# A four-layer graph network on one core: layer 0's gathered rows as three 16-bit pieces

## The reference, cut to what matters

```python
h = jnp.maximum(_layernorm(x, axis=-1), 0.0)
x = x + _L0_gnn_ref(h, edge_attr_128, src, dst, L0_gnn_W, L0_gnn_b, L0_gnn_We, L0_gnn_be)
# _L0_gnn_ref(nfeat, efeat, ...):
    h = nfeat * norm_src[:, None]                     # norm_src = out_degree ** -0.5
    agg = jax.ops.segment_sum(h[src], dst, num_segments=N)
    conv = agg @ W * norm_dst[:, None] + b
    sfeat = (nfeat @ W + b) / (in_deg + 1.0)[:, None]
    e = efeat @ We + be
    esum = jax.ops.segment_sum(e, dst, num_segments=N)
    return conv + sfeat + esum / jnp.clip(in_deg, 1.0, None)[:, None]
```

## Time and profile before

| | us |
|---|---|
| median of three runs | 7222.97 |
| lowest, highest | 7200.09, 7244.32 |
| span of the profiled execution | 7221.2 |

### The profile page before, as it was taken

How to read it: one execution, slowest core, us unless ns; L and a number is a source line. 1 busy time by engine, 2 the same in 40 slices (tenths; PEclk the granted TensorE clock), 3 DMA queues, 4 the chain that set the end, 5 groups by cost and what they waited for, 6 DMA issues and landing times. The chain is left out here.

```text
span 7221.2 us, 86037 instructions
## 1 busy us (share of the span) xinstructions
PE 4312.1 (60%) x19030; PEld 3495.4 (48%) x19030; DVE 3856.8 (53%) x11927; ACT 1462.0 (20%) x3928; POOL 4096.8 (57%) x4194
## 2 busy tenths in 40 slices
PE   4577777846656565795666666333344446556565
PEld 4466666635555555443444444233333345555554
DVE  7344444446666556745555555244444446556665
ACT  4122222212222222361111111000000112222222
POOL 1566666646666565006666665666666556555653
PEclk9877767666666666897888888555655566676766
DMA  2433333323333334164444445122222433333333
GB/s 49 125 99 101 100 100 101 100 89 105 106 108 108 105 108 87 64 279 140 130 136 128 136 129 117 52 55 61 59 56 59 72 100 107 110 113 105 113 115 64
DMA packets 426871, 738.64 MB, mean 102 GB/s; under 512 B 100571, under 2 KB 280628, under 8 KB 419797
## 3 DMA queue, kind: packets, MB, share of 16 engines
q0 software_dynamic: 173296, 436.67, 23.0%
q1 hardware_dynamic: 244484, 289.62, 12.3%
q10 hardware_dynamic: 8592, 6.82, 0.4%
HBM read 613.74 MB, written 120.20 MB: 102 GB/s over the span
## 5 line engine op out<-in xcount | busy, mean ns | idle before, releaser
L1619 POOL DMA_INDIRECT xh<-pair_d,src_i x1658 | 1653.2, 997 | 1181.9 <-issue 457.1
L2630 POOL DMA_INDIRECT l2e_rows<-msg_d,msg_i x829 | 807.1, 974 | 744.7 <-POOLq L61 316.8
L986 POOL DMA_INDIRECT l0e_rows<-node_d,src_i x832 | 793.9, 954 | 465.0 <-issue 220.6
L841 POOL DMA_INDIRECT l2f_rows<-msg_d,msg_i x829 | 787.0, 949 | 428.4 <-issue 231.2
L1141 PE MATMUL l0e_ps<-l0e_rows,l0e_sel 128*128 128x256 f32 x1664 | 787.1, 570 | 304.1 <-issue 187.3
L875 PE MATMUL l2f_ps<-l2f_rows,l2f_sel 128*128 128x128 f32 x1664 | 403.8, 409 | 597.2 <-DVE xh L906 482.6
L2748 PE MATMUL l2e_ps<-l2e_rows,l2e_sel 128*128 128x256 f32 x1664 | 485.8, 424 | 423.2 <-DVE l2e_sel L2842 406.4
L875 PEld LDWEIGHTS l2f_ps<-l2f_rows,l2f_sel 128*128 128x128 f32 x1664 | 359.1, 304 | 671.3 <-issue 409.6
L2807 DVE TENSOR_TENSOR l_acc<-l_acc,l2e_ps 128x256 f32 x832 | 349.2, 420 | 511.5 <-DMA node_d<-l1t_queries 347.7
L1206 DVE TENSOR_TENSOR early_acc<-early_acc,l0e_ps 128x264 f32 x832 | 356.6, 429 | 470.7 <-PE l0e_ps L1142 181.6
L906 DVE TENSOR_TENSOR xh<-xh,l2f_ps 128x128 f32 x832 | 238.2, 286 | 676.3 <-DMA tb_raw<-edges_d,starti 466.7
(11 more groups left out here) (454 smaller groups left out, 8155.1 us busy)
## 6 DMA issues: line engine op xcount, KB each, us to landing
l0e_rows<-in_edge_attr_dram SPq DMA_DIRECT2D x832, 64.0 KB
msg_d<-l1t_queries SPq DMA_DIRECT2D x50, 1024.0 KB, 3.9
l1te_local<-local_d SPq DMA_DIRECT2D x52, 512.0 KB
l2e_local<-local_d SPq DMA_DIRECT2D x52, 512.0 KB
l3te_local<-local_d SPq DMA_DIRECT2D x52, 512.0 KB
xh<-pair_d,src_i POOLq DMA_INDIRECT x1658
msg_d<-l2e_msg SPq DMA_DIRECT2D x50, 512.0 KB
l0e_rows<-node_d,src_i POOLq DMA_INDIRECT x832
```

Source lines behind the costliest of these rows:

```text
L841: pool.indirect_dma_start(rows[:, t % R, :], None, table, bass.IndirectOffsetOnAxis(index[:, t:t + 1], 0)) \
L986: pool.indirect_dma_start(rows[:, t % R, 0:D], None, table, bass.IndirectOffsetOnAxis(g.src_i[:, t:t + 1], 0)).then_inc(gathered[t % R], 16)
L1619: pool.indirect_dma_start(rows[:, t % R, :], None, g.pair_d, bass.IndirectOffsetOnAxis(g.src_i[:, t:t + 1], 0)).then_inc(gathered[n % RG], 16)
L2630: pool.indirect_dma_start(rows[:, t % R, :], None, table, bass.IndirectOffsetOnAxis(index[:, t:t + 1], 0)).then_inc(gathered[t % R], 16)
```

## The change

Table: a row of `node_d` becomes 384 16-bit numbers (768 bytes) instead of 128 32-bit ones (512 bytes): the value split into a head, a middle and a tail piece whose sum is exact, stored in the order middle, tail, head. After a slot is scaled, ScalarE copies the head to 16 bits, VectorE subtracts it, ScalarE copies the middle, VectorE writes the tail; SyncE sends the slot after its tail. The order on ScalarE is: (scale k,) head of k, middle of k-1; on VectorE: take the head from k, tail of k-1, scale k+1.

Pass: the ring is two, `near` (16-bit, 384 columns of pieces and 8 of relations, which `choose` now writes there) and `far` (32-bit, the edge features). Per tile PE makes one 16-bit product of 136 columns (head and relations), two of 128 columns that add to it, all with `narrow` as the stationary operand, and one 32-bit product of 128 columns. The edge sums now stand in columns 0 to 127 of the accumulator, the node sums in 128 to 255. `choose` waits for the summed tiles ahead of its first comparison. Some small buffers move into `g.coef`, which nothing uses in this pass.

```diff
@@ tables
+        spare = scratch[:, 24 * D:24 * D + 3 * 960].bitcast(BF16)
+        pieces = [spare[:, 1920 * b:1920 * (b + 1)].rearrange("p (w j f) -> p w j f", w=5, j=3) for b in range(3)]
+        pieces.append(g.mask[:, :, :, :].rearrange("p a b c -> p (a b c)")[:, 0:1920].rearrange("p (w j f) -> p w j f", w=5, j=3))
...
                 for k in range(K):
-                    if k in BY_ACT:
-                        sp.wait_ge(sent_a, 5 * (BY_ACT.index(k) + 1))
-                    else:
-                        sp.wait_ge(sent_d, len([j for j in range(k + 1) if j not in BY_ACT]))
+                    sp.wait_ge(tailed, k + 1)
                     sp.dma_start(g.node_d[k * 5 * P:(k + 1) * 5 * P, :].rearrange("(w p) f -> p w f", p=P),
-                                 hn[:, slot[k], :, :]).then_inc(hn_out[slot[k]], 16)
+                                 pieces[slot[k]].rearrange("p w j f -> p w (j f)")).then_inc(hn_out[slot[k]], 16)
...
+                def take_head(k):
+                    if k in BY_ACT:
+                        act.wait_ge(sent_a, 5 * (BY_ACT.index(k) + 1))
+                    else:
+                        act.wait_ge(sent_d, len([j for j in range(k + 1) if j not in BY_ACT]))
+                    nc.scalar.copy(pieces[slot[k]][:, :, 2, :], hn[:, slot[k], :, :]).then_inc(headed, 1)
+
+                def take_middle(k):
+                    act.wait_ge(left, k + 1)
+                    nc.scalar.copy(pieces[slot[k]][:, :, 0, :], hn[:, slot[k], :, :]).then_inc(middled, 1)
+
+                for k in range(K + 1):
+                    if k in BY_ACT:
+                        scale_rows(k)
+                    if k < K:
+                        take_head(k)
+                    if k >= 1:
+                        take_middle(k - 1)
...
+                def take_from(k):
+                    dve.wait_ge(headed, k + 1)
+                    nc.vector.tensor_tensor(hn[:, slot[k], :, :], hn[:, slot[k], :, :], pieces[slot[k]][:, :, 2, :],
+                                            ALU.subtract).then_inc(left, 1)
+
+                def take_tail(k):
+                    dve.wait_ge(middled, k + 1)
+                    nc.vector.tensor_tensor(pieces[slot[k]][:, :, 1, :], hn[:, slot[k], :, :], pieces[slot[k]][:, :, 0, :],
+                                            ALU.subtract).then_inc(tailed, 1)
+
+                for k in range(-1, K + 1):
+                    if 0 <= k < K:
+                        take_from(k)
+                    if k >= 1:
+                        take_tail(k - 1)
+                    if 0 <= k + 1 < K and k + 1 not in BY_ACT:
+                        scale_rows(k + 1)
@@ gather_first
-        rows = st.sb("rows", [P, R, 2 * D])
+        near, far = st.sb("near", [P, R, 3 * D + RELS], BF16), st.sb("far", [P, R, D])
...
-        of_rel = st.sb("of_rel", [P, 2, G, RELS])
...
-                    pool.indirect_dma_start(rows[:, t % R, 0:D], None, table,
+                    pool.indirect_dma_start(near[:, t % R, 0:3 * D], None, table,
...
-                            sp.dma_start(rows[:, r, D:2 * D], features[bass.ds(e0, P), :]).then_inc(loaded[r], 16)
+                            sp.dma_start(far[:, r, :], features[bass.ds(e0, P), :]).then_inc(loaded[r], 16)
...
-                    nc.tensor.matmul(ps[r % B][:, 0:2 * D], sel[:, r // G % 2, r % G, :], rows[:, r, :], start=True, stop=True)
-                    nc.tensor.matmul(ps[r % B][:, 2 * D:W0], sel[:, r // G % 2, r % G, :], of_rel[:, r // G % 2, r % G, :],
+                    few = narrow[:, r // G % 2, :, r % G]
+                    nc.tensor.matmul(ps[r % B][:, D:W0], few, near[:, r, 2 * D:], start=True, stop=False)
+                    for j in range(2):
+                        nc.tensor.matmul(ps[r % B][:, D:2 * D], few, near[:, r, j * D:(j + 1) * D], start=False, stop=(j == 1))
+                    nc.tensor.matmul(ps[r % B][:, 0:D], sel[:, r // G % 2, r % G, :], far[:, r, :],
                                      start=True, stop=True).then_inc(summed, 1)
...
                 def choose(n, b):
                     reach(dve, widened, n - 1)
+                    reach(dve, summed, G * (n - 1))
                     nc.vector.tensor_tensor(
                         narrow[:, b, :, :], dloc16[:, bass.ds(G * n, G)].unsqueeze(1).broadcast_to([P, P, G]),
                         numbers[:, :, :], ALU.is_equal)
-                    reach(dve, summed, G * (n - 1))
                     nc.vector.tensor_tensor(
-                        of_rel[:, b, :, :], g.rel[:, bass.ds(G * n, G)].unsqueeze(2).broadcast_to([P, G, RELS]),
+                        near[:, G * n % R:G * n % R + G, 3 * D:], g.rel[:, bass.ds(G * n, G)].unsqueeze(2).broadcast_to([P, G, RELS]),
```

More of the change, by code:

```diff
@@ L333, in tables @@
         (dv, built, counted, squared, evened, rooted, scaled, normed, asked, answered, scaled2, sent_a, sent_d,
-         laid, turned, taken, keyed, kept, out) = (
+         laid, turned, taken, keyed, kept, out, headed, left, middled, tailed) = (
             sem("tb_" + k) for k in ("dv", "built", "counted", "squared", "evened", "rooted", "scaled", "normed",
                                      "asked", "answered", "scaled2", "sent_a", "sent_d", "laid", "turned", "taken",
-                                     "keyed", "kept", "out"))
+                                     "keyed", "kept", "out", "headed", "left", "middled", "tailed"))
         got = [sem(f"tb_got{k}") for k in range(3)]
@@ L416, in _, with scale_rows @@
                 act.wait_ge(scaled2, 1)
-                for k in BY_ACT:
+                def scale_rows(k):
                     if turn_of[k]:
@@ L494, in _, with scale_rows @@
                 dve.wait_ge(normed, NW)
-                for k in range(K):
-                    if k not in BY_ACT:
-                        if turn_of[k]:
-                            dve.wait_ge(hn_out[slot[k]], 16 * turn_of[k])
-                        nc.vector.tensor_tensor(
-                            hn[:, slot[k], :, :], g.h[:, 5 * k * D:5 * (k + 1) * D].rearrange("p (w f) -> p w f", f=D),
-                            nsrc[:, 5 * k:5 * (k + 1)].unsqueeze(2).broadcast_to([P, 5, D]), ALU.mult).then_inc(sent_d, 1)
+                def scale_rows(k):
+                    if turn_of[k]:
+                        dve.wait_ge(hn_out[slot[k]], 16 * turn_of[k])
+                    nc.vector.tensor_tensor(
+                        hn[:, slot[k], :, :], g.h[:, 5 * k * D:5 * (k + 1) * D].rearrange("p (w f) -> p w f", f=D),
+                        nsrc[:, 5 * k:5 * (k + 1)].unsqueeze(2).broadcast_to([P, 5, D]), ALU.mult).then_inc(sent_d, 1)
+                def take_from(k):
[13 more added lines that the diff above has]
+                        scale_rows(k + 1)
 def make_masks(nc, g, dve, c):
@@ L955, in gather_first @@
         rstd, shift = st.sb("rstd", [P, 1]), st.sb("shift", [P, 1])
-        junk, hc, ht = st.sb("junk", [P, D]), st.sb("hc", [P, D]), st.sb("ht", [P, D])
-        vk, prod = st.sb("vk", [P, 2 * D]), st.sb("prod", [P, D])
+        junk, hc, ht = g.coef[:, 3 * D:4 * D], st.sb("hc", [P, D]), st.sb("ht", [P, D])
+        vk, prod = g.coef[:, 0:2 * D], g.coef[:, 2 * D:3 * D]
         ps = [st.ps(f"ps{b}") for b in range(B)]
@@ L1058, in scale_sums @@
                     nc.scalar.activation(ndst[:, :], part[:, 0:1], ACT.Sqrt).then_inc(rooted0, 1)
-                    nc.scalar.activation(z[:, 1, :], acc[:, bass.ds(v * W0 + D, D)], ACT.Copy,
+                    nc.scalar.activation(z[:, 1, :], acc[:, bass.ds(v * W0, D)], ACT.Copy,
                                          scale=part[:, 0:1]).then_inc(scaled0, 1)
@@ L1062, in scale_sums @@
                     act.nop(nofuse=True)
-                    nc.scalar.activation(z[:, 0, :], acc[:, bass.ds(v * W0, D)], ACT.Copy,
+                    nc.scalar.activation(z[:, 0, :], acc[:, bass.ds(v * W0 + D, D)], ACT.Copy,
                                          scale=ndst[:, 0:1]).then_inc(scaled0, 1)
@@ L2920, in gnn_stack @@
         g.keys_d = nc.dram_tensor("keys_d", (P + T * P + P,), F32, kind="Internal").ap()
-        g.node_d = nc.dram_tensor("node_d", (NP, D), F32, kind="Internal").ap()
+        g.node_d = nc.dram_tensor("node_d", (NP, 3 * D), BF16, kind="Internal").ap()
         g.pair_d = nc.dram_tensor("pair_d", (NP, 2 * D), F32, kind="Internal").ap()
```

## The result

The changed kernel takes 7261.09 us (median of 20 runs, 7233.2 to 7280.53) against 7222.4 us before (20 runs), a ratio of 1.0049 with an interval of 1.0037 to 1.006: slower by half a per cent, inside the range and near the forecast of 7245. The profiled execution spans 7263.7 us against 7221.2, 42.5 us more.

What follows compares the result with a forecast made beforehand. The prediction took the stream of gathers in layer 0's pass as the bound. Splitting +22, PE's relief -7 and longer rows +9 made +24 us on the median of 7222.97: 7247, given as 7245, range 7185 to 7305.

Steps and rivals of the forecast that it cites:

- The bound: Layer 0's pass: the stream of gathers sets the pace, 1.43 to 1.49 us each; PE, VectorE and ScalarE fit in.
- The rival in which PE is the bound: Layer 0's pass: pauses are PE's lag and go, -172 us, some 7070; 12% together with a middle course at 7160.
- The splitting, +22: End of the table stage: copies and subtractions making the pieces delay the first gather, costing 22 us.
- PE's relief, -7: Layer 0's pass: shorter PE tiles save 7 us, in the early part and the few longer steady periods.
- longer rows, +9: Layer 0's gathers: rows of 768 bytes in place of 512 cost 9 us over 832 gathers.
- the inference from the pair of stages with 512 and 1024-byte rows: Two other stages, 1.426 against 1.490 us a gather: doubling the row costs 0 to 0.064 us a gather.
- The rival of longer rows: Pauses in layer 0's pass grow with the bytes, 0.11 us a gather, +92 us, total 7330; chance 14%.
- PE's tile, 0.5 to 0.65 us: PE's products for one tile in layer 0's pass: 0.5 to 0.65 us at full clock against 0.66, twice that at half.
- The pauses: GpSimd in the pass's steady part: still eight gathers and a pause of about 2 us, sixteen gathers in 23.4 to 24.2.
- Everything after is the same, shifted by about 20 us: Stages after layer 0's pass: all unchanged, only about 20 us later.

Runs made afterwards that it cites:

- run 10: Changed kernel with two 16-bit products a tile in place of three and a 32-bit one, and no feature loads after the first 16 tiles: ratio to before 1.0004.
- run 4: Changed kernel with 256-byte rows, the head piece alone sent and gathered but multiplied three times: ratio to before 1.0024, pass 1271.0 us.
- run 9: Changed kernel with GpSimd's wait set for 12 of 16 ring slots in layer 0's pass, 16 of 32 in the later stage: ratio to before 1.0015.
- run 2: Changed kernel with two 16-bit products a tile in place of three and a 32-bit one, feature loads kept: ratio to before 1.0093, pass 1306.5 us.
- run 1: Changed kernel whose table stage makes only the head piece, the other two being zeros written once; pass unedited: ratio to before 1.0016.
- run 8: Changed kernel with two tiny GpSimd instructions after each gather, putting gathers 1.36 us apart: ratio to before 1.0069.
- run 6: Changed kernel with slots scaled two rounds ahead and scaled buffers freed by the tail that read them, not their send: ratio to before 1.0023.
- run 12: Changed kernel with the head piece alone, one 16-bit and one 32-bit product a tile, two tiny GpSimd instructions after each gather: 7204.71 us, ratio to before 0.9983.
- run 7: Changed kernel with one tiny GpSimd instruction after each gather: ratio to before 1.0053, pass 1258.3 us.
- run 11: Changed kernel with two 16-bit products a tile, all feature loads, and two tiny GpSimd instructions after each gather: ratio to before 1.0063, pass 1246.5 us.
- run 3: Changed kernel whose SyncE loads edge features for the first 16 tiles only, later tiles reusing them: ratio to before 1.0017.

## Why the prediction was right, and where it was not

*The bound.* Right in what it excluded: PE is not the bound. Taking a third of PE's tile (the change), more than half of it and the loads (run 10), two thirds of the rows' bytes (run 4), a quarter of the ring (run 9) or half of the other stage's ring (run 9) made the steady pace at most 0.04 us shorter or 0.013 longer; the light PE with its loads (run 2) made it 0.05 longer than in run 1 beside it. Spacing the gathers was paid out of the pauses (run 8). The rival in which PE is the bound, 7070 us, is refuted by runs 2 and 10. That the stream of gathers sets the pace is what is left, and the pauses, which grow with the gathers ahead of them, fit it; but the gathers' own transfers don't queue up (run 10), so the pauses' mechanism stays open. No run eased VectorE or ScalarE; against them as the bound stands only their busy time, 390 and 191 of 800 us. The paragraph Reading a trace of the Trainium skill's page "Trainium Kernel Development and Optimization", on which the prediction draws for this rival, stands there under Performance Expectations.

*The splitting, +22.* Measured 23.2. The end of the last tail came at 226.5 where I had 227, by two errors that cancel: a round takes 3.1 us and not 3.45 (a 16-bit copy is 0.72 us, and VectorE's steps, 0.82 us long, start 0.74 apart), and I had no term for the wait on a buffer's send, 2.94 us. Run 1 gives the shares, 17.2 and 6.0 us; run 6 shows that 11.9 of it were the order and not the work. That the sum came out within 1.2 us was luck.

*PE's relief, -7, and longer rows, +9.* Their sum, +2, met the 2.6 measured by luck, for both terms were wrong. Bytes cost 0 (run 4 against run 1), and of PE's relief nothing shows in the early part, where the prediction looked for it first: the first 104 gathers took 172.8 us against 173.0. The step that failed is the inference from the pair of stages with 512 and 1024-byte rows: run 4 shows no such cost between 256 and 768 bytes, so their 0.064 us are likely to come with the other work of those stages, which no run tested. The rule of the Trainium skill's page "DMA: Bandwidth & Descriptors" (Anatomy of one DMA), that a transfer pays for its bytes at 436 GB/s, would be an estimate of 0.15 us a gather between rows of 768 and 256 bytes if each byte were felt in the pace; run 4 shows nothing of it there. In the landing of a single gather the traces of runs 1 and 4 differ by 0.23 us (2.37 and 2.14). The rival of longer rows, 7330, falls with it.

*PE's tile, 0.5 to 0.65 us.* Mis-sized: 0.45 us at the full clock and 0.86 at the half. A 16-bit product comes every 0.06 us at the full clock (three from 926.13 to 926.30) and every 0.11 at the half (922.06 to 922.17), though each has its own weight load. The 0.107 us that the prediction took from the table stage is no half-clock figure: the granted clock is 1.00 there, in the kernel before.

```profile
183.90:187.40 3.50, 3.42 (x32) 3.14 (x32) 3.26 (x4) 0.00 (x0) 0.00 (x0) 1.00 0.00 0
```

Why products of 50 columns come more slowly there than those of 128 in the pass was not looked into; VectorE, which makes their operands, is busy for 3.26 of the 3.5 us. The lower figure, 0.17 us for three, was the right one. The error cost the forecast nothing, since PE is not the bound.

*The pauses.* "Eight gathers and a pause of about 2 us" was too rigid: half of the pauses now come after four gathers and last 1.35 us. Sixteen gathers take 23.78 us in the median, inside the 23.4 to 24.2 given, though only half of the single ones are.

*Everything after is the same, shifted by about 20 us.* Wrong for one stage. The stage with 1024-byte rows took 1231.9 to 1234.1 us in three kernels (before, runs 6 and 12), at a granted clock of 0.86, and 1245.6 to 1252.2 in five executions of four others (the changed kernel twice, runs 7, 8 and 11), at 0.83 to 0.84. The two executions of the changed kernel agree (1252.0 and 1248.9), so it may go with the kernel, though no line of that stage differs. That is 18 us of the 42.5 between the two profiles, and the likely reason why the result lies above 7245. Runs 1 to 4, 9 and 10 have 1253.8 to 1264.2 us at 0.82 to 0.84, on two chips from which there is no trace of the kernel before, so they don't decide it. Why the clock differs there was not found and not tested, and whether the clock makes the pace or follows it is open.

## What to carry to other kernels

A stage that is paced by one indirect gather after another gained next to nothing here from a faster TensorE or narrower rows; look at whether pauses and spacing add up to the same period before relieving another engine, which can even hurt (1306.5 us for the pass in run 2). A split into pieces is paid where the table is made, in a chain across two engines; working one slot further ahead, and freeing a buffer by its reader and not by its send, took half of that price back.

## What the runs showed of the hardware that I had not expected

While GpSimd issues gathers every 1.25 us without a pause, other work is held up: nine SyncE loads took 16.07 us to issue, single register moves of SyncE's 0.70 us instead of 0.03, and a hand-over from VectorE to ScalarE that takes 0.03 us otherwise had a median of 1.85 us from the ninth gather of a run on (run 2; in run 10 it was late in 6 of 25 such cases). The gathers' transfers are not what is late: each lands 2.1 to 2.4 us after its issue begins, early or late in a run. The gathers' long-run pace in a stage that does little else was 1.425 to 1.438 us in every run, with 32 or 16 slots.

A gather of 256 bytes a row costs GpSimd and the pass as much as one of 768 (947 and 949 ns of issuing in the median, 1271.0 and 1271.9 us for the pass, in runs 4 and 1), though it lands 0.23 us sooner.

The granted clock did not follow PE's time in flight: 1.00 with PE in flight for 278 to 295 of 800 us (runs 2, 10, 11), 0.71 with 487 and with 628 (the changed kernel and the one before), and 0.57 with 453 in run 12. Nor did the pass follow the clock: at 1.00 it took 1306.5, 1227.1 and 1246.5 us.
